# Windowed attention with 32 heads: one late copy of q's high parts, masks ahead of the rotation, and row maxima placed by small transfers

## The chip, the cores and the metric

The kernel runs on one core of a Trainium2 chip. Its engines are TensorE (PE, matmuls), VectorE (DVE), ScalarE (ACT), GpSimd (POOL) and SyncE (SP), which here only issues DMA transfers, each kind with an instruction queue of its own. The metric is the device time of one execution in microseconds. All intermediate data stay in SBUF, and TensorE writes to PSUM.

## The reference, cut to what matters

`x` is 8 x 512 x 256; 8 key/value heads serve 32 query heads of 64 columns, four query heads a group.

```python
xn = layernorm(x)
q = einsum('bqm,muh->bquh', xn, Wq) + bq;  k, v likewise with 8 heads
first  = even * cos - odd * sin            # interleaved rotation of q and k
second = odd * cos + even * sin
scores = einsum('bquh,bkuh->buqk', q * SCALE, k * SCALE)
scores = where(abs(pos_q - pos_k) <= 128, scores, -1e9)
probs  = softmax(concat([scores, sink]))[..., :-1]
s = einsum('buqk,bkuh->bquh', probs, v) @ Wo + bo
xq = (xn / scale).astype(float8_e4m3fn)    # scale from the largest |xn| of all
out = x + s * silu(xq @ weight.T + bias)
```

## The kernel before

**Steps and quarters.** The work is a software pipeline over 64 steps, one for each batch element and key/value group (`it = 8 * n + k`), with two filling steps ahead and one behind. Each step has four quarters `q`, one for each tile of 128 query positions. Within step `it`, TensorE projects the queries of step `it + 2` (quarter 0), forms the plain score rows of step `it + 1` (L1085, from which only each query's largest score is taken), forms the transposed scores of step `it` (L1108 and L1110, keys on the partitions), weighs the values with the exponentials (L1124), turns the head outputs (L1134) and projects them (L1147).

**Split numbers.** Scores are to have float32 accuracy, so each operand of the matmuls is split into a high part that the fast format holds exactly and a low remainder. `qT_full` holds, for 64 columns of q, the low parts on partitions 0 to 63 and the high parts on 64 to 127; against `kT_high`, which holds the keys' high parts twice, one matmul gives high x high and low x high (L1108). The third product needs q's high parts a second time, on partitions 0 to 63 of `qT_high`, against `kT_low` (L1110). Both q buffers have two halves, used by even and odd steps.

**The row maxima.** Before the exponential, each query's largest score is subtracted. VectorE finds it (L847), for two quarters (a pair) at a time, splits the negated maximum into two parts (`neg_parts`, 8 columns: two for each of four heads), TensorE turns these into 8 rows (L1067), and they are added by the same matmul L1110: `kT_low` has rows of ones on partitions 64 to 71, and `qT_high` has on partitions 64 to 71 the 8 rows. In a head's columns only its own two rows may be other than zero, so ScalarE copies the 8 rows four times, once for each head, each with a column of `own_rows` as scale that is one on the head's two rows and zero on the others (`max_rows`, L642 to L645). Pair 1 of step `it` is turned in quarter 0 of step `it`, pair 0 of step `it + 1` in quarter 2. The rows lie in PSUM bank `ring[2]`, which the turned head outputs need next: TensorE waits at L1209 and L1211 for ScalarE's copies.

**From projection to qT.** In a step, ScalarE takes the even and the odd columns out of PSUM (L616, L622), POOL rotates them (`turn_even` in quarter 0, `turn_odd` and `turn_rest` in quarter 1), ScalarE makes the high parts (`first_high` in quarter 1, `second_high` in quarter 2) and POOL the low ones (`first_low`, `second_low` in quarter 2). POOL also zeroes the corners of the exponentials that lie outside the window (`cut`, one or two blocks a quarter, L531), which the weighing of the next quarter needs. Within quarter 0, `turn_even` stands ahead of the mask, and waits until all six transfers of the step before have landed. Keys are made for four groups at once, twice in each batch element (k = 2 and 6): `keys_sum` in quarter 0 and `keys_low` in quarter 2 on POOL, `keys_high` in quarter 1 on ScalarE.

**SP's order.** SP executes its queue in order. In step `it` it sends the keys of step `t = it + 2` (six transfers of 64 KB, `keys_in`) and then the queries of step `a = it + 2` (`queries_in`): four transfers of 256 KB into `qT_full` (L376, L377) and two into `qT_high` (L381). `queries_in` first waits until the last score block of step `it` has been formed, since step `a` uses the same half. TensorE waits for the four and for the keys ahead of the first score row of the next step (L1074 to L1076). Where t is a multiple of four, the keys come from a freshly made group, and `keys_in` waits at L360 for POOL's `keys_low` of this same step. Results, and the loads of x, stand between at k = 0, 2 and 7.

```python
        sp.wait_ge(s_k_lo, 2 * quad + 2)               # L360, keys_in
        upto(sp, s_score_pe, NB * (a - 1))             # L372, queries_in; NB = 10 score blocks a step
        pool.wait_ge(s_even_done, a + 1)               # L468, turn_even
        upto(pool, s_qT_high_in, Q_IN * a)             # L471
```

## Time and profile before

| | |
|---|---|
| time, median of 3 runs | 2174.53 us (2162.39 to 2175.64) |
| profiled execution | 2158.91 us, its span 2157.2 us |
| granted TensorE clock, mean | 0.905 of full speed |
| busy: TensorE, VectorE, POOL, ScalarE | 85%, 59%, 47%, 41% of the span |
| DMA transfers of the kernel's queue | 44.6% of 16 engines' span |

The profile is one execution. Busy time of an engine is the time in its instructions; the rest it waits, for another engine's result or for a transfer. A timeline row gives the start, the duration, the engine, the line of the kernel, the operation with its output and inputs, and in brackets how long the engine had been idle before it and what ended that. "Issue" stands for an idle time whose end the profile ascribes to nothing. SPq is SP's issuing of transfers; the landing time of a transfer counts from its issue. A clock of 1.00 is 2.4 GHz, one of 0.50 is 1.2 GHz.

### The profile page before, as it was taken

Reading aid. Unit: us, or ns where it says so; the run is one execution under the profiler, and the core shown is the slowest. Engines: PE = TensorE matmul, PEld = TensorE weight load, DVE = VectorE, ACT = ScalarE, POOL = GpSimd, SP = SyncE. Lnnn points to the kernel's source line nnn. Section 1 sums busy time; section 2 is a strip of 40 time slices with the busy share of each in tenths; the row PEclk is TensorE's granted clock in tenths of the full one; section 3 lists DMA queues with packets and bytes.
Section 4 is the critical chain, followed back from the end, with each engine's and each line's share of the span. In section 5 each row is a group of like instructions: output and inputs, shape, how many; then the busy total and the mean of one; then the engine's idle time right before and its main releaser. Section 6 shows DMA issues by size and latency. Waiting matters only on the chain.

```text
span 2157.2 us, 33967 instructions
## 1 busy us (share of the span) xinstructions
PE 1823.1 (85%) x11139; PEld 1586.5 (74%) x11139; DVE 1272.2 (59%) x4156; ACT 886.5 (41%) x1893; POOL 1013.6 (47%) x1022
## 2 busy tenths in 40 slices
PE   2388888988989888988889888888898988898888
PEld 1177777777877777877777777777777777787777
DVE  8646556656656655655656655555665665565453
ACT  2134443444434444443444444343443444444343
POOL 4244444544635543553554554454463555355341
PEclk7579899999999988998999989898999998899899
DMA  4734443455255344445345344445425544534540
GB/s 151 129 47 59 62 67 59 79 84 70 40 85 77 64 65 68 68 61 91 52 60 94 57 64 67 63 76 84 65 43 87 77 66 63 74 56 58 91 64 13
DMA packets 92990, 150.89 MB, mean 70 GB/s; under 512 B 13712, under 2 KB 29840, under 8 KB 92816
## 3 DMA queue, kind: packets, MB, share of 16 engines
q1 hardware_dynamic: 92816, 148.72, 44.6%
q8 instruction: 91, 1.49, 0.3%
q14 instruction: 83, 0.68, 0.1%
HBM read 18.64 MB, written 4.19 MB: 11 GB/s over the span
## 4 chain that ended last, share of the span: by engine, by line
PE 48%; DMA 12%; issue 11%; POOL 9%; ACT 6%; SPq 5%; DVE 5%; POOLq 0%; DVEq 0%
PE pv_bank L1124 16%; DMA qT_high<-q_second_hi 7%; PE ring L1085 7%; PE acc L1147 6%; PE ring L1036 6%; PE score L1108 5%; PE score L1110 4%; DMA qT_full<-q_first_hi 4%; PE ring L1134 2%; POOL stage L531 2%; ACT qT_high L643 2%; ACT stage L610 2%; SPq L364 2%; SPq L376 1%; POOL q_second L473 1%
## 5 line engine op out<-in xcount | busy, mean ns | idle before, releaser
L847 DVE CUSTOM_DVE_ANT_0 junk<-ring,mask 128x384 bf16<-128x384 f32 (+1 forms) x1024 | 496.7, 488 | 696.5 <-PE ring L1085 687.7
L1124 PEld LDWEIGHTS pv_bank<-v,stage 128*128 128x128 f32 x5120 | 705.6, 206 | 30.2 <-issue 10.5
L1124 PE MATMUL pv_bank<-v,stage 128*128 128x65 f32 x5120 | 713.3, 282 | 10.8 <-ACT stage L610 3.8
L1085 PE MATMUL ring<-kT_high,qT_full 128*128 128x384 f32 (+1 forms) x1024 | 412.7, 404 | 219.6 <-issue 142.5
L610 ACT ACTIVATE stage<-score 128x512 f32<-128x512 f32 x640 | 356.8, 595 | 338.0 <-PE score L1110 337.3
L472 POOL TENSOR_TENSOR q_first<-q_even,cos 128x512 f32<-128x512 f32 x64 | 81.7, 1277 | 786.2 <-DMA qT_high<-q_second_hi 767.9
L1085 PEld LDWEIGHTS ring<-kT_high,qT_full 128*128 128x128 f32 x1024 | 213.7, 209 | 266.5 <-issue 178.7
L531 POOL TENSOR_SCALAR_AFFINE_SELECT stage<-stage 128x512 f32<-128x512 f32 x384 | 248.8, 663 | 232.5 <-ACT stage L610 231.5
L1108 PE MATMUL score<-qT_full,kT_high 128*128 128x512 f32 x640 | 279.6, 437 | 13.8 <-ACT stage L610 13.8
L643 ACT ACTIVATE qT_high<-ring,own_rows 8x256 fp32r<-8x256 f32 x512 | 196.3, 452 | 199.5 <-PE ring L1067 198.6
L1110 PE MATMUL score<-qT_high,kT_low 72*128 72x512 f32 x640 | 268.9, 420 | 0.0
L652 ACT ACTIVATE oT_hi<-ring 128x256 fp32r<-128x256 f32 x256 | 98.4, 384 | 391.1 <-PE ring L1134 391.1
L1108 PEld LDWEIGHTS score<-qT_full,kT_high 128*128 128x128 f32 x640 | 132.8, 207 | 66.4 <-ACT stage L610 49.0
L1036 PE MATMUL ring<-xT_hi,w_hi 128*128 128x512 f32 x320 | 142.8, 446 | 31.5 <-ACT q_even L616 22.6
L1147 PE MATMUL acc<-wo_hi,oT_hi 128*128 128x256 f32 x512 | 156.1, 305 | 0.5 <-DVE oT_lo L885 0.5
L1147 PE MATMUL acc<-wo_lo,oT_hi 128*128 128x256 f32 x512 | 155.7, 304 | 0.0
L1147 PE MATMUL acc<-wo_hi,oT_lo 128*128 128x256 f32 x512 | 155.1, 303 | 0.0
L1110 PEld LDWEIGHTS score<-qT_high,kT_low 72*128 72x128 f32 x640 | 132.3, 207 | 17.2
L885 DVE TENSOR_TENSOR oT_lo<-ring,oT_hi 128x256 fp32r<-128x256 f32 x256 | 108.7, 424 | 58.0 <-ACT oT_hi L652 53.8
L1036 PE MATMUL ring<-xT_hi,w_lo 128*128 128x512 f32 x320 | 127.8, 399 | 0.0
L1036 PE MATMUL ring<-xT_lo,w_hi 128*128 128x512 f32 x320 | 127.6, 399 | 0.0
L1134 PE MATMUL ring<-ident,o_norm 128*128 128x128 f32 x512 | 112.2, 304 | 18.0 <-ACT qT_high L643 17.3
(121 smaller groups left out, 2663.2 us busy)
## 6 DMA issues: line engine op xcount, KB each, us to landing
qT_full<-q_first SPq DMA_DIRECT2D x64, 256.0 KB, 4.2
qT_full<-q_first_hi SPq DMA_DIRECT2D x64, 256.0 KB, 5.6
qT_full<-q_second SPq DMA_DIRECT2D x64, 256.0 KB, 6.9
qT_full<-q_second_hi SPq DMA_DIRECT2D x64, 256.0 KB, 8.3
qT_high<-q_first_hi SPq DMA_DIRECT2D x64, 256.0 KB, 9.6
qT_high<-q_second_hi SPq DMA_DIRECT2D x64, 256.0 KB, 10.8
kT_high<-k_first_hi SPq DMA_DIRECT2D x128, 64.0 KB, 9.7
kT_high<-k_second_hi SPq DMA_DIRECT2D x128, 64.0 KB, 9.3
```

The lines of the kernel that those rows point to most:

```text
L531: nc.gpsimd.affine_select(out=pr, in_=pr, compare_op=ALU.is_ge, fill=0.0, base=0, pattern=[[0, GROUP], [sign, P]], channel_multiplier=-sign) \
L610: nc.scalar.activation(prob[:, q % 2 * 3 + n, :], score[(FIRST[q] + n) % 2][:, :], ACT.Exp) \
L643: last = nc.scalar.activation(qT_high[D:D + NR, s % 2, h, pair * 2 * P:(pair + 1) * 2 * P], ring[2][0:NR, 0:2 * P], ACT.Copy, scale=own_ro ...
L847: nc.vector.tensor_tensor_reduce(junk[:, h % 2, 0:cols], ring[h % 2][:, 0:cols], mask[:, m0:m0 + cols], 1.0, LOWEST, ALU.add, ALU.max, row ...
L885: nc.vector.tensor_tensor(oT_lo[:, q % 2, :], ring[2][:, 0:KT * P], oT_hi[:, q % 2, :].bitcast(F32), ALU.subtract).then_inc(s_oT_lo_done, 1)
L1036: last = nc.tensor.matmul(ring[1][:, :], w[:, k, col:col + P], xs[:, k, :], start=(n == 0), stop=(n == len(products) - 1))
L1085: nc.tensor.matmul(ring[h % 2][:, 0:cols], qT_full[:, b % 2, h, q * P:(q + 1) * P], kT_high[:, b % 3, k0 * P:k0 * P + cols], start=True, s ...
L1108: nc.tensor.matmul(score[blk % 2][:, :], kT_high[:, c % 3, k * P:(k + 1) * P], qT_full[:, c % 2, :, q * P:(q + 1) * P], start=True, stop=F ...
L1110: nc.tensor.matmul(score[blk % 2][:, :], kT_low[0:D + NR, c % 3, k * P:(k + 1) * P], qT_high[0:D + NR, c % 2, :, q * P:(q + 1) * P], start ...
L1124: last = nc.tensor.matmul(pv[:, h, :], prob[:, q % 2 * 3 + n, h * P:(h + 1) * P], v[:, slot, k, :], start=(n == 0), stop=(n == len(BLOCKS[ ...
L1134: last = nc.tensor.transpose(ring[2][:, k * P:(k + 1) * P], o_flat[:, k * P:(k + 1) * P], ident[:, :])
L1147: last = nc.tensor.matmul(acc[q // 2][:, (q % 2) * M:(q % 2 + 1) * M], left[:, q % 2, k * P:(k + 1) * P], right[:, col:col + M], start=fre ...
```

## The change

**The second copy of the high parts** is no longer two transfers from `q_first_hi` and `q_second_hi` behind the other four. SP copies partitions 64 to 127 of `qT_full` to 0 to 63 of `qT_high` in one transfer of 512 KB (`highs_in`), first thing in the next step, once the four have landed. `turn_even` no longer waits for the second copy, only for the four.

**The order on SP** becomes: high parts of step it + 1, keys (t not a multiple of four), small transfers for pair 1 of step it, result, small transfers for pair 0 of step it + 1, queries, keys (t a multiple of four), result.

**The row maxima.** ScalarE copies the 8 turned rows once, into `turned_rows`, when the small transfers of the pair before have landed. SP then sends each head's two rows (2 KB) to their place in `qT_high` (`rows_in`, four transfers). The other rows of `qT_high` on partitions 64 to 95 are zeroed once at the start by VectorE. TensorE's scores wait for the four transfers. `own_rows` and its two masks go.

**The order on POOL and ScalarE.** POOL masks quarter 0 ahead of `turn_even`; `first_low` and `second_low` follow `turn_rest` in quarter 1, `keys_sum` moves from quarter 0 to 2 and `keys_low` from 2 to 3. ScalarE's `second_high` moves from quarter 2 to 1 and `keys_high` from 1 to 3.

```diff
@@ SP
-                upto(sp, s_qT_high_in, Q_IN * a)
-                for row, _, high, _, _ in parts:
-                    sp.dma_start(qT_high[row:row + HALF, a % 2, :, :].bitcast(F32), high[:, :]) \
-                        .then_inc(s_qT_high_in, 16)
+            def highs_in(b):
+                sp.wait_ge(s_qT_first_in, Q_IN * (b + 1))
+                sp.wait_ge(s_qT_second_in, Q_IN * (b + 1))
+                upto(sp, s_qT_high_in, 16 * b)
+                sp.dma_start(qT_high[0:D, b % 2, :, :].bitcast(F32), qT_full[D:2 * D, b % 2, :, :].bitcast(F32)) \
+                    .then_inc(s_qT_high_in, 16)
+            def rows_in(s, pair):
+                sp.wait_ge(s_max_rows_done, 2 * s + pair + 1)
+                if s == 0 and pair == 0:
+                    sp.wait_ge(s_ones_ready, 3)
+                for h in range(GROUP):
+                    sp.dma_start(qT_high[D + 2 * h:D + 2 * h + 2, s % 2, h, pair * 2 * P:(pair + 1) * 2 * P]
+                                 .bitcast(F32), turned_rows[2 * h:2 * h + 2, :]).then_inc(s_rows_in, 16)
@@ SP, step
+                if real(b):
+                    highs_in(b)
                 if real(t) and t % QUAD:
                     keys_in(t)
+                if real(it):
+                    rows_in(it, 1)
                 if k == 0 and n >= 1:
                     result(n - 1, 0)
+                if real(it + 1):
+                    rows_in(it + 1, 0)
+                if real(a):
+                    queries_in(a)
                 if real(t) and t % QUAD == 0:
                     keys_in(t)
-                if real(a):
-                    queries_in(a)
@@ POOL
-                upto(pool, s_qT_high_in, Q_IN * a)
...
-                    if q == 0 and new_keys:
-                        keys_sum(quad)
-                    if q == 0 and real(a):
-                        turn_even(a)
-                    if q == 1 and real(a):
-                        turn_odd(a)
-                    if q == 2 and real(a):
-                        first_low(a)
-                    if real(it):
-                        cut(it, q)
-                    if q == 1 and real(a):
-                        turn_rest(a)
-                    if q == 2 and real(a):
-                        second_low(a)
-                    if q == 2 and new_keys:
-                        keys_low(quad)
+                    if q == 1 and real(a):
+                        turn_odd(a)
+                    if real(it):
+                        cut(it, q)
+                    if q == 0 and real(a):
+                        turn_even(a)
+                    if q == 1 and real(a):
+                        turn_rest(a)
+                        first_low(a)
+                        second_low(a)
+                    if q == 2 and new_keys:
+                        keys_sum(quad)
+                    if q == 3 and new_keys:
+                        keys_low(quad)
@@ ACT
-                for h in range(GROUP):
-                    last = nc.scalar.activation(qT_high[D:D + NR, s % 2, h, pair * 2 * P:(pair + 1) * 2 * P],
-                                                ring[2][0:NR, 0:2 * P], ACT.Copy, scale=own_rows[:, h:h + 1])
-                last.then_inc(s_max_rows_done, 1)
+                upto(act, s_rows_in, 16 * GROUP * (2 * s + pair))
+                nc.scalar.activation(turned_rows[:, :].bitcast(F32R), ring[2][0:NR, 0:2 * P], ACT.Copy) \
+                    .then_inc(s_max_rows_done, 1)
...
-                    if q == 2 and real(a):
-                        second_high(a)
...
                     if q == 1 and real(a):
                         first_high(a)
-                    if q == 1 and k in (2, 6) and quad < BATCH * QUADS:
+                        second_high(a)
+                    if q == 3 and k in (2, 6) and quad < BATCH * QUADS:
                         keys_high(quad)
@@ DVE, once
+            nc.vector.memset(qT_high[D:D + HALF, :, :, :].bitcast(F32), 0.0).then_inc(s_ones_ready, 1)
@@ PE, scores
-                    pe.wait_ge(s_qT_high_in, Q_IN * (c + 1))
+                    pe.wait_ge(s_qT_high_in, 16 * (c + 1))
-                    pe.wait_ge(s_max_rows_done, 2 * c + q // 2 + 1)
+                    pe.wait_ge(s_rows_in, 16 * GROUP * (2 * c + q // 2 + 1))
```

## Rows read from the trace of the kernel before

**Rows 1.** The page, part 1: engine, busy us, share of the span, instructions

```profile
PE 1823.1 (85%) x11139; PEld 1586.5 (74%) x11139; DVE 1272.2 (59%) x4156; ACT 886.5 (41%) x1893; POOL 1013.6 (47%) x1022
```

**Rows 2.** The waits: engine, line, what ended them, us in total, times, longest

```profile
POOL q_first L472 <- DMA qT_high<-q_second_hi: 767.9, 61, 17.5
PE ring L1085 <- issue: 142.5, 49, 7.1
PE ring L1134 <- ACT qT_high L643: 17.3, 47, 0.8
```

**Rows 3.** Timeline of an ordinary step: start, us, engine, line, operation, [idle before, releaser]

```profile
1008.71 0.40 PE L1110 MATMUL score<-qT_high,kT_low 72*128 72x512 f32 x1
...
1009.14 0.58 SPq L376 DMA_DIRECT2D qT_full<-q_first  x1
1011.06 0.61 SPq L377 DMA_DIRECT2D qT_full<-q_second_hi  x1
...
1019.38 0.36 PE L1085 MATMUL ring<-kT_high,qT_full 128*128 128x256 f32 x1 [1.98 <-issue]
```

**Rows 4.** Transfers of two steps, at 1102 and 1009: issuer, count, KB each, us to landing

```profile
qT_full<-q_second_hi SPq DMA_DIRECT2D x1, 256.0 KB, 8.3
kT_low<-k_second SPq DMA_DIRECT2D x1, 64.0 KB, 2.1
...
qT_high<-q_second_hi SPq DMA_DIRECT2D x1, 256.0 KB, 11.1
kT_low<-k_second SPq DMA_DIRECT2D x1, 64.0 KB, 8.6
```

**Rows 5.** Timeline of a fourth step, with the first and last of fifteen such waits

```profile
216.98 0.55 PE L1085 MATMUL ring<-kT_high,qT_full 128*128 128x256 f32 x1 [5.02 <-issue]
...
1101.26 1.28 POOL L511 TENSOR_TENSOR k_second<-k_second,k_second_hi 128x512 f32<-128x512 f32 x1
1101.61 0.40 PE L1110 MATMUL score<-qT_high,kT_low 72*128 72x512 f32 x1
1102.57 0.50 SPq L364 DMA_DIRECT2D kT_high<-k_first_hi  x1
1106.36 0.58 SPq L376 DMA_DIRECT2D qT_full<-q_first  x1
...
1116.64 0.55 PE L1085 MATMUL ring<-kT_high,qT_full 128*128 128x256 f32 x1 [5.94 <-issue]
...
2009.87 0.55 PE L1085 MATMUL ring<-kT_high,qT_full 128*128 128x256 f32 x1 [5.68 <-issue]
```

**Rows 6.** Timeline, ScalarE and the first score block of quarter 2

```profile
1000.14 0.63 ACT L627 ACTIVATE q_first_hi<-q_first 128x512 fp32r<-128x512 f32 x1
1004.60 1.53 ACT L643 ACTIVATE qT_high<-ring,own_rows 8x256 fp32r<-8x256 f32 x4 [0.85 <-PE ring L1067]
1011.86 0.38 ACT L652 ACTIVATE oT_hi<-ring 128x256 fp32r<-128x256 f32 x1 [2.09 <-PE ring L1134]
...
1030.26 0.39 PE L1108 MATMUL score<-qT_full,kT_high 128*128 128x512 f32 x1
```

**Rows 7.** Stretches with columns: busy us of each engine, granted clock, DMA share, GB/s

```profile
1019.10:1023.10 4.00, 3.27 (x24) 3.10 (x24) 1.37 (x7) 2.23 (x7) 0.00 (x0) 0.82 1.06 141
1114.00:1124.00 10.00, 7.36 (x33) 7.20 (x34) 3.58 (x13) 2.13 (x6) 3.45 (x4) 0.50 0.76 101
```

**Rows 8.** Timeline, POOL's first rotation of an ordinary step

```profile
1023.68 1.28 POOL L472 TENSOR_TENSOR q_first<-q_even,cos 128x512 f32<-128x512 f32 x1 [13.60 <-DMA qT_high<-q_second_hi]
```

**Rows 9.** Groups by line: matmuls of the weighing, busy us, mean ns, idle before by releaser

```profile
L1124 PE MATMUL pv_bank<-v,stage 128*128 128x65 f32 x5120 | 713.3, 282 | 10.8 <-ACT stage L610 3.8 <-DVE v L836 3.8 <-issue 1.8
```

**Rows 10.** Timeline of the start: DVE and SP

```profile
1.17 1.34 DVE L979 MEMSET kT_low<- 32x1536 f32 x1 [1.17 <-PEq L1301]
...
62.87 0.60 SPq L350 DMA_DIRECT2D x_res<-in_x  x1
...
74.73 1.41 DVE L711 BATCH_NORM_STATS2 stats<-x_res 128x6 f32<-128x256 f32 x4 [14.41 <-DMA x_res<-in_x]
```

20 lines of the change are left out of this document (7 added, 13 removed).

## The prediction

> **What bounds the kernel now.** I read the page's engine totals first, then the table of waits, then the timeline of a few steps, then the landing times of the transfers, and last the granted clock by windows. TensorE is busy for 85% of the span [rows 1]. No other engine is close, so a change is worth what it does to TensorE's own waits. POOL's wait of 768 us for the second q copy [rows 2] is the largest wait of all, and TensorE hardly feels it. Of TensorE's waits one stands out: 142.5 us in 49 waits ahead of the score rows L1085, released by nothing the profile names [rows 2]. The timeline names it. In an ordinary step the last score block starts at 1008.71 and takes 0.40, so it ends at 1009.11. SP issues the first q transfer 0.03 us later, because line 372 waits for exactly that block. The fourth is issued at 1011.06, and the rows start at 1019.38 after 1.98 us of idling [rows 3]. The fourth transfer lands 8.3 us after its issue [rows 4]: 1011.06 + 8.3 = 1019.36. So each step has a fixed distance of 10.3 us from the end of the last score block to the first row, of which TensorE's own work fills 8.3.
>
> Every fourth step the distance is longer. There SP must first send a group's keys: k_low ends at 1102.54, six key transfers go out from 1102.57, and the first q transfer leaves at 1106.36, 4.35 us after the last score block's end at 1102.01. The rows start at 1116.64, after a wait of 5.94 us. There are 15 such waits, the first 5.02 and the last 5.68 [rows 5], 83.8 us together. The other 34 make 58.7.
>
> **The change, part by part.**
>
> *Keys behind queries.* SP now sends q first and the fourth step's keys last, and the keys' conversion and low part move to quarter 3. q leaves at S + 0.03 (S is the end of the last score block) and has landed at S + 10.3. The keys: ScalarE reaches their conversion behind the head outputs of that quarter, which end 3.1 us after S in the ordinary step (1011.86 + 0.38), and two conversions of 0.63 take it to S + 4.4 [rows 6]. Two POOL subtractions of 1.28 [rows 5] take it to S + 6.95. Six issues at the spacing 0.64 put the last at about S + 10.15. On an empty queue a key transfer lands in 2.1 us, behind the q ones in 8.6 [rows 4]. The queue is empty of q by S + 10.3, so the last keys land at S + 12.2. Today's rows start at S + 14.6 here, and about 14.1 over the fifteen. Gain 1.9 x 15 = 28 us, taken as 27. Bounds: nothing, if something holds the keys 2 us longer; 83.8 - 15 x 2.0 = 54 us, if they come no later than q.
>
> *The clock.* After the wait of 5.9 us the granted clock is at its lower level, 1.2 GHz (0.50), for all of 1114 to 1124; around the 2 us wait it is 0.82 over four microseconds [rows 7]. A wait of 3.9 lies between. Most of those slow microseconds are no loss, since the rows there are paced by the maxima too. I take 0.3 us a time, 4 us; bounds 0 and 15 x 2.5 = 37 if a shorter wait keeps the full clock.
>
> *One ScalarE copy for four.* Four masked copies take 1.53 us together [rows 6], 0.38 each in the row; I allow 0.45 for a lone one. TensorE waits for them ahead of the head transposes 47 times, 17.3 us in all, never above 0.8 [rows 2]. 1.08 us less ends every one: 17 us. Bounds 15 and 18.
>
> *Four small transfers.* Each moves 2 KB. No row shows one; the issues shown take 0.50 to 0.61 us, whether of 64, 256 or 512 KB [rows 3, 5, 10], with 0.64 from one to the next, and a lone one of 64 KB lands in 2.1. For pair 0 the ScalarE copy starts at 1004.60 [rows 6], 4.5 us ahead of S. Copy 0.45 and four issues of 0.64 leave SP free for q 1.4 us before S. So nothing, hidden behind quarter 2's remaining matmuls; the cover is gone at 1.0 us an issue. For pair 1 the order on SP is: the q copy (issued when q has landed, S + 10.35), six keys in three steps of four (to S + 14.8), then the four (to S + 17.4), landing by about S + 19.5. TensorE wants them at 1030.26 [rows 6], which is S + 21.15. Cover about 1.7 us, so nothing again; in the fourth steps there are no keys in between and the cover is larger.
>
> *The second q copy, one transfer of 512 KB, a step later.* The sixth of today's q transfers is issued 1.3 us after the fourth and lands 11.1 us after its issue [rows 4], so the last two take 2.0 us each, 131 GB/s; at that rate it takes 4 us, S + 10.35 to about S + 16.5, while nothing else is wanted. Its reader is a step away. The Trainium skill, "SBUF — State Buffer", section on the DMA port swizzle, says partitions 0 to 31 and 32 to 63 share ports, so a transfer into 64 partitions has only half of them. By that rule the joined copy gains nothing in rate from its shape, and the sum stays as it is; whether it loses by reading only half the ports as well no run here shows. At half of today's rate it would end at S + 19 and push the four small transfers to about S + 21, just at the end of their cover, so the far bound is 0.5 us x 45 = 22 us.
>
> *Masking ahead of the rotation on POOL.* Today the rotation waits 13.60 us for the second copy and the quarter-0 mask stands behind it [rows 8]. TensorE's whole wait ahead of the weighing L1124 is 10.8 us, of which 3.8 is VectorE's values and 3.8 the exponentials [rows 9]. I take 3 us; bounds 0 and 7. The rotation starts 4 us sooner. What is late next is the second high part, now in quarter 1 on ScalarE: POOL delivers it at about S + 21.0, it ends at 21.65, and the next exponential is wanted at S + 22. Cost 0, bound 0.6 x 64 = 40 us if POOL is a microsecond slower. Where the low parts waited behind a mask they are now earlier; they were ready before S anyway.
>
> *Start and end.* The load of x that VectorE awaits for 14.41 us is issued at 62.87 behind six q transfers [rows 10]; two of those now come later: 2 x 2.0 = 4 us less. Behind the keys it may be issued 1 us later. The new memset is 4096 against 1536 columns at 1.34 us [rows 10], 3.5 us, of which 1 to 2 stand ahead of the first statistics. Net 3 us gained, bounds -3 and +6. The end is untouched.
>
> **Sum:** 27 + 4 + 17 + 3 + 3 = 54 us. The profiled execution took 2158.9 (span 2157.2), so it would become about 2105. The median of the runs is 2174.5, with 2162.4 the lowest; waits taken away subtract alike, so the median becomes **2120**.
>
> **The rivals.**
>
> *B, the keys only change places.* TensorE waits for keys as long as it waited for q behind keys. For it: the keys start 6.4 us later after S than today, and depend on ScalarE's last operation of the quarter. Against: the key transfers are short. Then 2174.5 - 23 = 2151. 15%.
>
> *C, slower: the small transfers hold SP.* The four for pair 0 stand directly ahead of q in SP's queue, in every step. If an issue of two rows takes 1.3 us and not 0.64, q leaves 4 x 1.3 + 0.45 - 4.5 = 1.2 us after S, and all of it reaches the 62 steps: 72 us, and pair 1 misses its cover as well, by about 1 us in 45 steps. It decides from 1.0 us an issue. 2120 + 72 = 2192, with the second part up to 2235. Against: every issue shown lies between 0.50 and 0.61 whatever its size [rows 3, 5, 10]. The Trainium skill, "DMA: Bandwidth & Descriptors", section on why a DMA increments its semaphore by 16, says that a transfer over two partitions runs on two engines and the issuing sequencer writes the other 14 increments itself. By that rule SP has extra work in each issue; no row here has such a transfer. 11%.
>
> *D, the gains don't add up.* VectorE's maxima and the clock take back what the copies give. For it: VectorE is busy for 59% of the span and sits in the loop of every row [rows 1]. About 2168, the gain under 1%. 12%.
>
> *E, q itself lands sooner.* If the two transfers now queued behind q slowed it, the 58.7 us of ordinary waits shrink too, and the clock stays up: 2120 - 50 = 2070. Against: two that follow take the same 2.0 us as those before them, in order. 10%.
>
> **How the numbers follow.** The forecast has 52%, the others as given. Range: the forecast's own is 2095 to 2145 (keys gain 0 to 54, ScalarE bound). To hold 8 in 10 it takes in B and most of D and a piece of E: 2078 to 2168. About 1% (22 us) is what a measurement of this kernel can tell. Faster by over 1%: forecast, E, and half of B, 0.70. Within: half of B, D, and a little of C, 0.20. Slower: 0.10.
>
> **What would show it.** After the change: POOL's wait at L472 down from 768 to under 600 and on a qT_full transfer; no TensorE wait for the max rows; first q transfer 0.03 us after S in all steps; waits ahead of L1085 of about 3.9 us in the fourth steps and an unchanged 2.0 elsewhere. Wrong would be: q issued later than S + 0.1 (C), fourth-step waits of 6 us (B), a new wait ahead of the first score block of quarter 2 (small transfers late), or ScalarE idling for q_second ahead of the exponentials.

## The result, and the profile after

| | before | after |
|---|---|---|
| time, median of 4 runs each | 2171.67 us (2162.39 to 2175.64) | 2068.95 us (2054.21 to 2074.46) |
| ratio | 1 | 0.9522, 95% interval 0.9463 to 0.9581 |
| profiled execution, span | 2158.91, 2157.2 us | 2074.46, 2072.7 us |
| granted TensorE clock, mean | 0.905 | 0.907 |

The kernel became 103 us faster. The forecast was 2120, its range 2078 to 2168, so the result lies below the range. A second run of the same kernel beside the first experiments gave 2078.24 us, ratio 0.9586 (0.9512 to 0.9661); it is named below where a comparison needs it. Ratios leave out two executions (one of the kernel before, one of a kernel below) that lay over 1.5% above the fastest of the same kernel.

I read the profile after in the order of the one before. First the engine totals, which answer to [rows 1]:

```profile
PE 1807.7 (87%) x11139; PEld 1592.2 (77%) x11139; DVE 1277.2 (62%) x4157; ACT 730.8 (35%) x1509; POOL 1011.2 (49%) x1019
```

ScalarE has lost 384 instructions and 156 us, the copies. POOL's busy time is the same. Then the waits, which answer to [rows 2] (line numbers are about 8 higher for TensorE, 11 for POOL):

```profile
POOL stage L542 <- ACT stage L619: 833.7, 193, 18.7
...
PE ring L1093 <- DMA kT_low<-k_second: 71.0, 16, 8.5
...
POOL q_first L483 <- DMA qT_full<-q_second_hi: 86.6, 45, 3.0
```

```profile
PE ring L1093 <- issue: 39.6, 31, 5.1
PE ring L1075 <- issue: 26.2, 39, 1.1
```

POOL's wait of 768 us ahead of the rotation has moved to the masks, which now stand ahead of it. TensorE's 142.5 us in 49 waits ahead of the score rows have become 71.0 + 39.6 = 110.6 in 47, and its waits for the ScalarE copy are gone. One line has grown: L1075, the turn of the row maxima, 18.7 to 26.2 us. I had not looked at it before.

The fourth step, timeline (start, us, engine, line, operation):

```profile
946.83 0.40 PE L1118 MATMUL score<-qT_high,kT_low 72*128 72x512 f32 x1
...
947.26 0.61 SPq L376 DMA_DIRECT2D qT_full<-q_first  x1
949.21 0.61 SPq L377 DMA_DIRECT2D qT_full<-q_second_hi  x1
...
952.73 1.29 POOL L522 TENSOR_TENSOR k_second<-k_second,k_second_hi 128x512 f32<-128x512 f32 x1
...
957.13 0.59 SPq L366 DMA_DIRECT2D kT_low<-k_second  x1
...
959.49 0.55 PE L1093 MATMUL ring<-kT_high,qT_full 128*128 128x256 f32 x1 [4.00 <-DMA kT_low<-k_second]
```

S, the end of the last score block, is 947.23. The first q transfer leaves at S + 0.03, the key subtraction ends at S + 6.8, the last key is issued at S + 9.9 and the row starts at S + 12.3, after a wait of 4.00 us. This is the forecast's course to within 0.3 us (3.9, S + 6.95, S + 10.15, S + 12.2). The landings (the page's part 6: issuer, count, KB each, us to landing):

```profile
qT_high<-qT_full SPq DMA_DIRECT2D x64, 512.0 KB, 4.5
qT_full<-q_first SPq DMA_DIRECT2D x64, 256.0 KB, 4.2
...
qT_full<-q_second_hi SPq DMA_DIRECT2D x64, 256.0 KB, 8.0
```

And the view that led to the cause which no part of the sum had, VectorE's groups by line. Before:

```profile
L862 DVE CAST neg_parts<-neg_max 128x8 fp32r<-128x8 f32 x128 | 48.1, 376 | 4.4
```

After:

```profile
L869 DVE CAST neg_parts<-neg_max 128x8 fp32r<-128x8 f32 x128 | 100.8, 787 | 4.4
```

The same copy of eight columns took 376 ns on average before and takes 787 now. It is one of four small VectorE operations (L865 to L872) between the last row maximum of a pair of quarters and TensorE's turn of the maxima; I call them the chain, and say that it is caught where one of them is held up by an operation of POOL. The first pair's chain follows quarter 1's rows, the second pair's follows quarter 3's. Timeline of a first-pair chain after, VectorE, then POOL:

```profile
1094.52 0.29 DVE L865 SCALAR_TENSOR_TENSOR neg_max<-row_max,neg_sink 128x8 f32<-128x8 f32 x1
1094.84 1.22 DVE L869 CAST neg_parts<-neg_max 128x8 fp32r<-128x8 f32 x1
1095.98 0.15 DVE L870 TENSOR_TENSOR sink_arg<-neg_max,neg_sink 128x8 f32<-128x8 f32 x1
1096.10 0.56 DVE L872 TENSOR_TENSOR neg_parts<-neg_max,neg_parts 128x8 fp32r<-128x8 f32 x1
1096.58 0.61 DVE L840 TENSOR_TENSOR v<-ring,v_bias 128x448 f32<-128x448 f32 x1
```

```profile
1094.75 1.28 POOL L507 TENSOR_TENSOR q_second<-q_second,q_second_hi 128x512 f32<-128x512 f32 x1
1095.99 1.23 POOL L542 TENSOR_SCALAR_AFFINE_SELECT stage<-stage 128x512 f32<-128x512 f32 x2
```

The CAST starts 0.09 us behind a POOL subtraction of two operands and ends with it (1096.06 and 1096.03). Sorted by what POOL does at its start, the 128 CASTs of the trace after take 0.17 us beside an idle POOL (51 of them), 0.37 beside a mask (2), and 1.22 beside a product or subtraction of 128x512 (75: the second low part L507 in 60 first-pair chains, the keys' low part L522 in 15 second-pair ones). Before, 69 had POOL idle, 13 a mask, 43 a 128x512 sum, product or difference at 0.7 on average (all in the first pair) and 3 a small operation.

The CAST alone understates what POOL did in the kernel before. In 21 of those 43 chains it had begun ahead of POOL's operation and was short, and the operation behind it was held up:

```profile
1093.93 0.75 DVE L858 SCALAR_TENSOR_TENSOR neg_max<-row_max,neg_sink 128x8 f32<-128x8 f32 x1
1094.71 0.17 DVE L862 CAST neg_parts<-neg_max 128x8 fp32r<-128x8 f32 x1
1094.79 1.25 DVE L863 TENSOR_TENSOR sink_arg<-neg_max,neg_sink 128x8 f32<-128x8 f32 x1
1095.96 0.15 DVE L865 TENSOR_TENSOR neg_parts<-neg_max,neg_parts 128x8 fp32r<-128x8 f32 x1
```

```profile
1093.38 1.27 POOL L485 TENSOR_TENSOR q_odd<-q_odd,cos 128x512 f32<-128x512 f32 x1
1094.73 1.28 POOL L487 TENSOR_TENSOR q_second<-q_second,q_odd 128x512 f32<-128x512 f32 x1
```

So the whole chain is the measure. From the start of its first operation to the end of its last, the first pair's takes 2.08 us on average before and 2.30 after, the second pair's 0.57 before and 0.96 after. The collision was there already; the change has not taken it away.

The Trainium skill, "SBUF — State Buffer", section "Who interferes with whom", states the rule: VectorE and GpSimd share a pair of SBUF ports, a VectorE instruction in a two-port mode or with two SBUF inputs takes it, and whoever comes second is blocked until the other's instruction is over. The trace agrees: the blocked CAST and the blocked difference end as POOL's operation does (the 1.25 us one at 1096.04, POOL's at 1096.01), not in proportion to their eight columns.

### The profile page after: what moved, and what is told of

Its sections match the earlier page's. It is cut to its first block, busy times and chain, and to the rows that moved or that the text cites. A ratio compares the mean times of both kernels' runs of the same rounds, so it can differ in the third digit from the quotient of the medians.

```text
span 2072.7 us, 34158 instructions
## 1 busy us (share of the span) xinstructions
PE 1807.7 (87%) x11139; PEld 1592.2 (77%) x11139; DVE 1277.2 (62%) x4157; ACT 730.8 (35%) x1509; POOL 1011.2 (49%) x1019
## 4 chain that ended last, share of the span: by engine, by line
PE 68%; issue 6%; DVE 6%; SPq 5%; ACT 4%; DMA 4%; POOL 3%; POOLq 0%; DVEq 0%
PE pv_bank L1132 23%; PE ring L1093 10%; PE acc L1155 8%; PE ring L1044 8%; PE score L1116 7%; PE score L1118 6%; PE ring L1142 3%; SPq L364 3%; ACT stage L619 2%; PE ring L1053 2%; DMA qT_full<-q_second_hi 2%; DMA kT_low<-k_second 2%; POOL k_first L520 1%; POOL k_second L522 1%; SPq L366 1%
## 5 line engine op out<-in xcount | busy, mean ns | idle before, releaser
L1044 PEld LDWEIGHTS ring<-xT_hi,w_hi 128*128 128x128 f32 x320 | 63.5, 199 | 71.7 <-ACT q_even L625 42.4
L886 DVE TENSOR_TENSOR o_norm<-pv_bank,rden 128x256 f32<-128x256 f32 x256 | 108.7, 425 | 9.3 <-DVE rden L883 0.5
```

Of the source, the lines that this page charges most:

```text
L886: nc.vector.tensor_tensor(o_norm[:, :, :], pv[:, :, 0:D], rden[:, :].rearrange("p (h a) -> p h a", a=1).broadcast_to([P, GROUP, D]), ALU.m ...
L1044: last = nc.tensor.matmul(ring[1][:, :], w[:, k, col:col + P], xs[:, k, :], start=(n == 0), stop=(n == len(products) - 1))
```

## The experiments

Each kernel ran in three rounds beside the kernel before on the same chip, so ratios to it are the measure. A difference between two kernels is given as the difference of their ratios times 2170 us; with intervals of 0.2 to 0.8% to either side it is good to some 10 to 20 us. The changed kernel stands at 0.9522 in the result and at 0.9586 in its repeat: against the repeat, every gain over after is 14 us larger and every loss 14 us smaller. In the sections on parts, "on after" means that one part of the change is undone, "on before" that one is made alone.

### What each part is worth

**The changed kernel again**, no edit: 0.9586, as told above.

> The changed kernel unaltered, timed on the same chip beside the kernel before and the three undoings. Expected by every theory: about 2069 us, 0.952 of before, with row waits of 3.95 to 4.8 us in the fourth steps and 1.75 us in the ordinary ones.

**Keys part undone, on after** (keys sent ahead of the queries, their sum in quarter 0, low part in 2, high in 1):

```
-                if real(a):
-                    queries_in(a)
                 if real(t) and t % QUAD == 0:
                     keys_in(t)
+                if real(a):
+                    queries_in(a)
```

> The changed kernel with the keys' part undone: in the fourth steps SP sends the keys ahead of the queries again, and keys_sum, keys_high and keys_low stand in quarters 0, 1 and 2. Theory T (each part is worth the TensorE wait that it takes away, plus a share of clock, and the parts add up): the fifteen fourth-step waits go back from 4.2 to about 5 to 6 us, so 15 to 27 us of waits and 5 us of clock, 2090 to 2100. Rival R (the surplus over my sum comes from coupling, POOL being early lets everything else run freely): POOL is now early anyway, so k_low is ready well before the last score block, q leaves on time or at most 1 us late, and the undoing costs under 8 us: below 2077.

Measured 2048.67 us (2032.36 to 2055.99), ratio 0.9441 (0.9364 to 0.9517): 18 us faster than after, 31 than its repeat on the same chip, each to some 20 us. The part that the forecast gave the largest term gains nothing in the changed kernel; by both comparisons it is rather a loss. With the new order of the queries' work the keys' low part ends 3.7 us ahead of S on average, q leaves between S + 0.03 and S + 2.7 (1.2 on average), and the fourth steps' wait is 3.04 us, less than the 4.2 of after. The keys' low part also leaves the second pair's chain, whose mean falls from 0.96 to 0.57 us.

**Four copies again, on after** (the one copy and the small transfers undone, the four masked copies back):

```
-                nc.scalar.activation(turned_rows[:, :].bitcast(F32R), ring[2][0:NR, 0:2 * P], ACT.Copy)
+                for h in range(GROUP):
+                    last = nc.scalar.activation(qT_high[D:D + NR, s % 2, h, pair * 2 * P:(pair + 1) * 2 * P],
+                                                ring[2][0:NR, 0:2 * P], ACT.Copy, scale=own_rows[:, h:h + 1])
```

> The changed kernel with the row maxima's part undone: ScalarE makes four masked copies again and there are no small transfers. Theory T: the 17 us of TensorE waits ahead of the head transposes come back, 2069 + 17 = 2086, with up to 5 us more of clock. Rival R (ScalarE's relief also shortened other waits, so that this part is worth 30 us or more): 2100 or more. Rival S (the small transfers hold SP and cost what the copies give): 2069 or less.

Measured 2120.25 us (2105.12 to 2127.94), ratio 0.9773 (0.9698 to 0.9847): 54 us slower than after, 41 slower than its repeat on the same chip. This is more than theory T's 2086; the time is rival R's.

**Second copy behind q again, on after**, as two transfers, with POOL's wait for them at the odd half's product:

```
+                if real(a):
+                    highs_in(a)
...
-                if real(b):
-                    highs_in(b)
```

> The changed kernel with the second copy of q's high parts as before: two transfers of 256 KB from q_first_hi and q_second_hi right behind the queries (in the fourth steps behind the keys); POOL waits for them ahead of turn_odd, not ahead of turn_even, and the mask stays ahead of the rotation. Theory T (q lands 0.25 us sooner and never a whole microsecond late, because nothing is queued behind it): ordinary row waits go back from 1.75 to 2.0 us with some of 3.0, the 34 waits from 39 to 59 us, 2069 + 20 = 2089. Rival R (the second copy mattered only through POOL's wait and the mask): row waits stay at 1.75 us, and the time at 2069 to 2075.

Measured 2127.94 us (2118.94 to 2138.27), ratio 0.9818 (0.9747 to 0.9889), 64 us slower than after, 50 slower than the repeat. In the two of every eight steps with the longest ordinary waits these went from 1.73 to 2.37 us on average, and the fourth q transfer lands 8.3 us after its issue, not 8.0: two transfers queued behind q do slow q. All ordinary waits went from 39.6 to 56.7 us, as theory T had them; its time of 2089 was 39 us too low. The time at the half clock is about 395 us here and about 320 in after (the measure is that of the section on waits below); why is not traced further.

**Keys part alone, on before:**

```
-                if real(t) and t % QUAD == 0:
-                    keys_in(t)
                 if real(a):
                     queries_in(a)
+                if real(t) and t % QUAD == 0:
+                    keys_in(t)
```

> The kernel before with the keys' part alone: in the fourth steps SP sends the queries first and the keys last, keys_sum, keys_high and keys_low stand in quarters 2, 3 and 3. Theory T2 (the keys' part is judged against POOL's lateness: it only pays where POOL is late, so the parts don't add up): fourth-step waits go from 5.6 to about 4 us, 15 x 1.6 = 24 us of waits and some clock, 2172 - 30 = 2142. Rival (the part costs 25 us whatever stands around it, as its undoing on the changed kernel suggests): 2172 to 2200.

Measured 2182.21 us (2175.01 to 2192.67), ratio 1.0085 (1.0054 to 1.0117), slower. TensorE's waits:

```profile
PE ring L1085 <- DMA kT_low<-k_second: 125.6, 16, 11.3
PE ring L1085 <- issue: 59.1, 34, 5.2
```

The keys now stand behind six q transfers and not four, and the fourth steps wait 7.6 us for them on average. This is rival B of the prediction, in a kernel without the late second copy, and the rival of this run.

**Queries' order on POOL and ScalarE undone, on after** (rotation ahead of the quarter-0 mask, low parts and the second high part in quarter 2):

```
+                    if q == 0 and real(a):
+                        turn_even(a)
                     if q == 1 and real(a):
                         turn_odd(a)
+                    if q == 2 and real(a):
+                        first_low(a)
                     if real(it):
                         cut(it, q)
-                    if q == 0 and real(a):
-                        turn_even(a)
                     if q == 1 and real(a):
                         turn_rest(a)
-                        first_low(a)
-                        second_low(a)
+                    if q == 2 and real(a):
+                        second_low(a)
```

> The changed kernel with the order on POOL and ScalarE of before for the queries: the rotation ahead of the quarter-0 mask, first_low and second_low around the quarter-2 mask, second_high in quarter 2. Keys and transfers as changed. Theory T2 (the mask's place is worth little, because the rotation now starts 4 us sooner by itself): no waits ahead of the weighing come back, 2075 to 2082. Rival (the order is where the surplus over my sum sits, through ScalarE's wait for the second high part ahead of the third exponentials): 2095 or more.

Measured 2015.5 us (2008.21 to 2027.13), ratio 0.9309 (0.9248 to 0.937): 46 us faster than after; neither theory nor rival had it. Of the first-pair CASTs 7 are now held up by a 128x512 difference and 18 stand beside a mask, where 60 were held up, and the chain's mean is 1.43 us, not 2.30. The second pair's 15 are caught as in after, at the keys' low part.

**The two transfer parts alone** (late second copy, one copy with small transfers):

> Keeps the joined late second copy and the one ScalarE copy with small transfers; the keys and the order of the queries' work on POOL and ScalarE stand as before the change. Theory (each of the two reorders costs by itself, keys about 27 us, queries' order about 57 us): 2072 - 27 - 57, about 1990 us, with the fourth steps' first q transfer at S + 1.2 and their row waits near 3.0 us, VectorE's negation chain back near 1.5 us. Rival (both reorders load the same POOL, so that undoing the second gives nothing more): 2010 to 2015 us, the time of the better of the two alone.

Measured 2037.38 us (2035.82 to 2038.39), ratio 0.9387 (0.9355 to 0.942). Neither theory had it. Set beside the runs above it shows that the parts don't add: on these two the keys part gives 17 us (0.9387 to 0.9309), beside the new order it costs 18 (0.9441 to 0.9522); the new order costs 12 without it (0.9387 to 0.9441) and 46 with it. The gap of 34 us between these is good to some 26; the 17, 18 and 12 by themselves are hardly more than the intervals leave open.

**The late second copy alone, on before:**

> The kernel before with the late, joined second copy alone. Theory (the late second copy frees POOL's turn of the queries, so the fourth steps' keys are ready before S, and the queue behind q is shorter): fourth-step waits from 5.6 us to about 3, 15 x 2.6 = 39 us and the clock with them, so 2170 - 50 = 2120 or less. Rival (the gain of the late copy exists only beside the new order on POOL): within 15 us of the time before, 2155 to 2175, with the keys' low part still ending after S + 0.4.

Measured 2054.77 us (2044.99 to 2068.34), ratio 0.948 (0.9418 to 0.9542), 113 us faster than before by itself. The way that the theory gave is wrong: the keys are no earlier (low part at S - 0.8, q at S + 3.2 on average; before, S - 0.6 and S + 3.4) and the fourth steps still wait 5.0 us. POOL's rotation starts at S + 10.1 in ordinary steps and not at S + 14.2, and the first pair's chain takes 1.18 us on average and not 2.08.

**One copy and small transfers alone, on before:**

> The kernel before with one ScalarE copy and small transfers alone; the two second copies stay behind the queries and POOL waits for them as before. Theory (TensorE's wait for the maxima's rows goes, 17.3 us, and the clock and the rows behind it give about as much again): 2170 - 35 to 45, about 2130. Rival one (the copies are worth only their 17 us as in the forecast): 2153. Rival two (the small transfers stand ahead of q in SP's queue and cost what the copies give): 2170 or above.

Measured 2157.1 us (2152.12 to 2157.83), ratio 0.9929 (0.9908 to 0.9951): 15 us. Rival one, the forecast's 17, is the nearest.

So, in the order in which the parts were stacked: late second copy -113, one copy and small transfers -20, keys -17, new order on POOL and ScalarE +46; together -104 us.

### POOL beside VectorE's chain

**POOL's second low part behind the chain, on after.** One wait more, nothing moved:

```
                 pool.wait_ge(s_second_hi, a + 1)
+                upto(pool, s_neg_done, 2 * (a - 1) + 1)
                 nc.gpsimd.tensor_tensor(q_second[:, :], q_second[:, :], q_second_hi[:, :], ALU.subtract)
```

> The changed kernel with one wait added: POOL's subtraction for the second low part waits until VectorE's four small operations on the negated maxima of pair 0 are done. The order on every engine stays. Theory (POOL's 128x512 subtraction and VectorE's small operations with two operands in SBUF exclude each other; 60 of 64 of the chains of pair 0 are caught, 1.05 us each, and TensorE and its clock pay more than once over): CAST mean from 0.79 to about 0.3 us, time 2069 - 50, about 2015 to 2025. Rival (the order of mask and rotation costs by making the mask or the exponentials late, and the stretched operations are a mere sign): 2060 to 2075, with the CAST short all the same.

Measured 1986.72 us (1973.52 to 1992.05), ratio 0.9151 (0.9101 to 0.9201): 80 us faster than after, from a wait, and 30 below the theory, which had counted the CAST alone. The same place in the step, VectorE, then POOL:

```profile
1036.24 0.29 DVE L866 SCALAR_TENSOR_TENSOR neg_max<-row_max,neg_sink 128x8 f32<-128x8 f32 x1
1036.56 0.17 DVE L870 CAST neg_parts<-neg_max 128x8 fp32r<-128x8 f32 x1
1036.64 0.16 DVE L871 TENSOR_TENSOR sink_arg<-neg_max,neg_sink 128x8 f32<-128x8 f32 x1
1036.77 0.17 DVE L873 TENSOR_TENSOR neg_parts<-neg_max,neg_parts 128x8 fp32r<-128x8 f32 x1
```

```profile
1037.09 1.29 POOL L508 TENSOR_TENSOR q_second<-q_second,q_second_hi 128x512 f32<-128x512 f32 x1 [0.58 <-DVE neg_parts L873]
```

From the start of the first operation to the end of the last the chain takes 0.70 us here and 2.14 in the timeline of after; over all first pairs 0.76 and 2.30. POOL idles 0.58 us for it, and its result is wanted only at S. TensorE's wait at the turn of the maxima, 26.2 us in after, is gone but for 1.9 us at one place.

**A useless POOL product beside the chain, and the same behind it**, on the kernel with the queries' order undone:

```
+                    if q == 1 and real(it + 1):
+                        beside_chain(it + 1)
...
+                pool.wait_ge(s_max_done, TILES * GROUP * b + 2 * GROUP)
+                nc.gpsimd.tensor_tensor(pool_junk[:, :], cos[:, :], sin[:, :], ALU.mult)
```

The second kernel waits for `s_neg_done, 2 * b + 1` instead.

> The kernel with the order of mask, rotation and low parts as before the change (2015.5 us) and one useless POOL product of 128x512 a step, which starts when the last maximum of pair 0 is there, beside VectorE's small operations. Theory: the chain is caught in about 63 steps, CAST mean near 0.7 us, time 2015 + 40 to 55, about 2060. Rival (small operations' length is off the path): 2015 to 2022.

> As the run with the useless product beside the chain, but the product waits until the chain is done. Same work on POOL, some tenths of a us later. Theory: the chain is free, 2015 to 2025 us. Rival (POOL's extra 1.3 us a step costs by itself): the same as with the product beside the chain.

Measured 2121.28 us (2118.32 to 2133.28), ratio 0.9791 (0.9743 to 0.9839), beside the chain; 1994.25 us (1989.73 to 2000.66), ratio 0.9196 (0.9147 to 0.9245), behind it. The work is the same, the place differs by a microsecond, and 129 us lie between. The CAST's group, first beside, then behind:

```profile
L880 DVE CAST neg_parts<-neg_max 128x8 fp32r<-128x8 f32 x128 | 95.6, 747 | 4.4
```

```profile
L880 DVE CAST neg_parts<-neg_max 128x8 fp32r<-128x8 f32 x128 | 37.8, 296 | 4.4
```

Beside it TensorE waits at the turn of the maxima:

```profile
PE ring L1086 <- issue: 43.4, 45, 1.7
```

Behind it the kernel is even 25 us faster than without the useless product (0.9196 against 0.9309): waiting for the chain also takes the real differences out of its way, none of the 64 first-pair chains is caught. 129 us is more than the theory's 55; over 64 chains it is 2.0 us each. In the trace beside the chain each chain meets not only the useless product but also the first low part behind it, which holds the CAST in 48 of them, and the whole chain takes 2.65 us on average against 0.57 behind it, 2.08 us more. TensorE's waits of the 43.4 us line are gone behind the chain but for 0.9 us, and the time at the half clock is about 400 us beside it and about 220 behind it; half of that difference is 90 us. So the cost is in part TensorE's wait and in larger part the slow matmuls behind it.

The first pair's chain from its first start to its last end, and how many of the 64 take over 1 us:

| kernel | mean, us | over 1 us | ratio |
|---|---|---|---|
| before | 2.08 | 56 | 1 |
| before, only POOL's wait moved (below) | 1.28 | 32 | 0.9688 |
| before, late second copy | 1.18 | 25 | 0.948 |
| two transfer parts | 1.32 | 31 | 0.9387 |
| after without the queries' order | 1.43 | 37 | 0.9309 |
| after | 2.30 | 61 | 0.9522 |
| after, low part behind the chain | 0.76 | 7 | 0.9151 |
| useless product beside the chain | 2.65 | 63 | 0.9791 |
| useless product behind it | 0.57 | 0 | 0.9196 |

Between kernels that differ only in where POOL's work meets the chain (the last four rows, pairwise) time and chain move together; across kernels with other transfers the chain is one term among several.

**Only POOL's wait moved, on before** (all transfers stay):

```
 def turn_even(a):
-                upto(pool, s_qT_high_in, Q_IN * a)
...
 def turn_odd(a):
                 pool.wait_ge(s_odd_done, a + 1)
+                upto(pool, s_qT_high_in, Q_IN * a)
```

> The kernel before with a single edit: POOL's wait for the second q copy stands ahead of the odd half's product in quarter 1, where its buffer is first written, and no longer ahead of the even half's in quarter 0. All transfers stay as before. Theory (the late second copy was worth 115 us by itself because POOL's rotation and the quarter-0 mask came 4 us earlier, out of the way of VectorE's chain): most of it, 2060 to 2090 us. Rival (it was worth that because two transfers less stand behind q in SP's queue): within 20 us of before, 2150 to 2175.

Measured 2101.88 us (2093.23 to 2107.69), ratio 0.9688 (0.9642 to 0.9733): between theory and rival, nearer to the theory. 68 us of the late copy's 113 come from POOL's work being 4 us earlier. The first-pair chains that take over 1 us fall from 56 to 32, and their mean by 0.80 us, 51 us over 64 steps; TensorE's waits ahead of the rows fall by 9 us and those ahead of the weighing from 10.8 to 0.4. The other 45 us (good to some 17) come with the two transfers off q's queue: TensorE's waits ahead of the rows are 133.7 us here and 116.0 with the late copy, and in the ordinary steps with the longest waits (two of every eight) they fall from 2.4 to 1.76.

**The guard put into the kernel before:**

```
+                upto(pool, s_neg_done, 2 * (a - 1) + 1)
                 nc.gpsimd.tensor_tensor(q_odd[:, :], q_odd[:, :], cos[:, :], ALU.mult)
```

> The kernel before with one wait added and nothing moved: POOL's last two operations of the rotation (and so the first low part behind them) wait until VectorE's small operations on the maxima of pair 0 are done. POOL still waits for the second q copy in quarter 0. Theory (the overlap is the cost): 2170 - 60 to 90, about 2095, below what the earlier wait for the second copy gave. Rival (the late rotation makes the high and low parts and with them q's transfers late): 2150 or above, with the first q transfer no longer 0.03 us behind the last score block.

Measured 2278.88 us (2270.05 to 2284.41), ratio 1.0525 (1.0484 to 1.0567), 114 us slower, although no first-pair chain is caught. The time lies where the rival had it, "2150 or above", but not by its mechanism: q still leaves at S + 0.03 in the ordinary steps. Both missed the queue behind the product. The waits of this kernel:

```profile
PE ring L1135 <- ACT qT_high L644: 125.3, 103, 2.3
```

```profile
ACT q_second_hi L632 <- POOL q_second L488: 156.7, 63, 4.8
```

```profile
POOL q_odd L486 <- DVE neg_parts L866: 156.1, 63, 7.2
```

POOL's rotation is delayed behind the chain; ScalarE's second high part waits for it, and in ScalarE's order the copies of the row maxima stand behind that. TensorE waits for them 125.3 us, where it was 17.3 [rows 2]. A wait is free only where its product has slack. On after the product was the second low part, wanted two quarters later; here it was one that ScalarE was about to ask for.

### What a wait of TensorE costs beyond its length

**Useless matmuls in the row waits, on after.** They compute nothing and begin when the wait does: 17 of 512 columns in the fourth steps, 6 in two of the other four of every eight.

```
+                    if q == 0 and real(b) and b % 8 in (0, 4, 5, 6) and b > 1:
+                        idle_filled(b, 17 if b % 4 == 0 else 6)
                     row(0)
```

> The changed kernel with useless matmuls in TensorE's idle time ahead of the first score row: 17 of 512 columns (3.7 us) in the fourth steps, 6 (1.3 us) in the two classes of steps with a 1.75 us wait. They write a bank that the score row overwrites; nothing else is changed and no work is saved. Theory C (the granted clock multiplies each wait: 169 of the 321 slow microseconds follow these waits and cost 0.3 to 0.65 us each): the clock stays at 2.4 GHz through these quarters, slow time falls by 130 us or more, and the time by 40 to 80 us, to 2000 to 2035. Rival D (the slow microseconds lie beside VectorE's maxima and cost nothing, the surplus is elsewhere): 2070 to 2080, or above if the matmuls overrun.

Measured 2021.19 us (2017.29 to 2030.38), ratio 0.9335 (0.9269 to 0.9402): 41 us less than after, with no transfer earlier: theory C's range. The mean granted clock rose from 0.907 to 0.946. Summed over windows of one microsecond from 115 us on, the time at the half clock fell from about 320 to about 150 us; half of the difference, 85 us, is what that stretch of matmuls takes less, and part of it lies beside other waits.

**Real work put there instead** (the output product and the first weighing ahead of row 0 of quarter 0):

> The changed kernel with useful work moved into the same idle time: in quarter 0 the output projection (6 matmuls, 1.4 us) and the first head's weighing go ahead of the first score row. Theory C: the ordinary waits of 1.75 us vanish, the fourth-step waits fall from 4.1 to 2.3, 34 + 27 = about 60 us of idle, and half as much again by the clock: 2075 - 90 = 1985. Rival D (idle time only): 2075 - 60 = 2015. Rival F (VectorE's maxima start no sooner and become the bound): 2060.

Measured 2064.76 us (2050.13 to 2066.93, and 2084.84 in the execution left out), ratio 0.9513 (0.944 to 0.9586), no change. The waits ahead of row 0 (from step 1 on) fall from 102.0 to 61.1 us, but the first score block of quarter 2 now waits for the small transfers of the row maxima, where after had 1.8 us in 4 waits:

```profile
PE score L1116 <- DMA qT_high<-turned_rows: 24.4, 24, 2.2
```

The rows start later behind the work put ahead of them, and with them the maxima. That this is what makes the small transfers late is argued, not tested. Rival F's 2060 is the nearest.

**The filler on the two transfer parts, and on the guarded kernel** (11 and 6 matmuls, 17 and 6):

> The kernel with the transfers only, and useless matmuls of 512 columns in TensorE's row waits: 11 in the fourth steps and 6 in two of the other four of every eight, each begun only when the wait begins; they compute nothing. Theory (a wait costs its length and then a stretch at the half clock): less slow clock, about 30 to 45 us below the same kernel without them, so 1945 to 1960. Rival (the clock falls for another reason than these waits, and the matmuls delay the rows): the same time or 10 us more.

> The best one so far (POOL's second low part behind VectorE's small operations, 1986.7 us) with useless matmuls of 512 columns in TensorE's row waits: 17 in the fourth steps, 6 in two of the other four of every eight, begun only when the wait begins; they compute nothing. Theory (each wait costs its length and then slow clock): 48 us less as in the two pairs run before this, 1935 to 1950. Rival (with the chain free there is little slow clock left to win): 1970 to 1987.

Measured 1989.08 us (1983.18 to 1992.48), ratio 0.9162 (0.9126 to 0.9198), and 1936.14 us (1934.42 to 1937.83), ratio 0.8935 (0.8909 to 0.8962). The filler gives 41, 49 and 47 us on three kernels, the last as the theory had it. The last one beats both kernels of the case, by 231 and 127 us. Span and clock of the guarded kernel without and with it:

```profile
core 0: 1987.5 us, clock 0.929
```

```profile
core 0: 1936.1 us, clock 0.964
```

## Why the prediction was wrong, point by point

**The step that failed first** is the part on the second q copy: a step later, "while nothing else is wanted", it was counted only for its own transfer time, and POOL's wait of 768 us for it was put down as one that "TensorE hardly feels". Leaving q's queue was worth 113 us by itself and stood in the sum with 0. TensorE does not feel the wait. It feels where POOL's work lands after it. POOL's rotation, masks and low parts fill about 14 us a step, and the wait pushed the rotation's end to where VectorE prepares the maxima. The trace of before showed it, in the CAST's mean of 376 ns for eight columns against 178 for a reciprocal of four, and more plainly in the first pair's chain of 2.08 us beside the second pair's of 0.57. I costed only queues and results, not what two engines do to each other while both have work. 68 us of the 113 come with POOL's earlier work, by the run that moved the wait alone; the shorter chains (51 us) and fewer waits ahead of rows and weighing make them up.

**What that leaves of the sum.** In the changed kernel the collision is back: its first-pair chain takes 2.30 us, so what the late copy took out of the chain the new order put in again, and the two don't show in the total. In the profiled executions the gain is 84 us, where the sum had 54. TensorE's waits account for most of it: 21 in the fourth steps, 19 in the ordinary ones, 17 for the copies, 10 ahead of the weighing, 5 at the start, less 7 at the turn of the maxima. The ordinary waits are the term that stood at nothing. Some 19 us are not traced.

**Rival E was real.** The other 45 us came with the two transfers gone from behind q; 18 of them are waits ahead of the rows. I gave it 10% on the ground that transfers go in order. Those that follow do slow the earlier ones: the fourth q transfer lands 8.0 us after its issue, not 8.3, and the ordinary waits went from 58.7 us in 34 to 39.6 in 31.

**Masking ahead of the rotation, +3:** wrong in sign. The weighing's wait did go, from 10.8 us [rows 9] to 0.6, but it is 0.6 too with the mask behind the rotation in the changed kernel, and 0.4 with the late copy alone: POOL's earlier start ended it, and the mask's place gave nothing. And the low parts, which the text called "now earlier; they were ready before S anyway", landed on the chain's CAST in 60 of 64 steps, and the group cost 46 us. With one wait more the same order is at 0.9151, against 0.9309 with the old one without the wait; but the old order whose chain is free, useless product and all, is at 0.9196, so that the new order itself gains is not shown.

**The keys, 27 us:** the course was right to 0.3 us, and the fourth steps' waits fell from 83.9 to 62.5 us. With the earlier POOL and the old order the measured gain is 17. In the changed kernel as it is the part came out as a loss of 18 us, near the edge of the intervals; what it was priced against, the fourth steps' low part ending on average only 0.6 us ahead of S, is no longer true there: without the part it ends at S - 3.7 and the fourth steps wait 3.04 us, not 4.2. I priced against the old timing a part that stands beside another part which changes it.

**One copy for four, 17 us:** measured 15 alone, 20 on the late copy, 41 to 54 in the changed kernel. TensorE's wait for it is gone, as forecast. Why undoing it costs so much more there is not settled; the time at the half clock goes from about 320 to about 375 us with it, and half of the difference, 27 us, is a part.

**The small transfers, 0, and rival C:** the cover held. An issue takes 0.58 us on average (0.61 for a q transfer), q leaves at S + 0.03 in all steps, and TensorE waits 1.8 us for them, in 4 waits. The cover is thin, as reckoned: with other work ahead of the rows the waits for them were 24.4 us. The Trainium skill, "DMA: Bandwidth & Descriptors", in the section on why a DMA increments its semaphore by 16, had the issuing sequencer write increments itself; in the issues' length this does not show.

**The clock, 4 us:** the mean clock did not move (0.905 to 0.907), so the term was about right in the sum and by chance. Its price was not: I took a wait to cost little beyond its length, and filling waits with matmuls gave 41 us for waits that did not become shorter.

**Rate of the joined copy:** 512 KB between two ranges of 64 partitions land in 4.5 us where 256 KB of a q transfer need 4.2, so it loses nothing, and the bound of 22 us fell away. The start gained 5.3 us (first row of step 1 at 109.0, before 114.3), 3 forecast; with the keys part undone it is at 113.6, with the late copy alone at 111.0, so the parts don't add here either.

**The range** was 90 us wide and all its cases took after's gains as a sum over queues. None had POOL and VectorE excluding each other, and that moved the time by up to 129 us in the runs above, more than the whole forecast of 54.

## What to carry to other kernels

Look for an instruction whose mean duration is too long for its shape: if a small VectorE operation in a chain that TensorE waits for is longer than its like, lay POOL's timeline beside it, time the whole chain and not one of its operations, and hold POOL's two-operand work back until the chain is done, but only work whose result has slack and has no engine's queue behind it. Price each part of a change against the timeline that the other parts leave, not the old one. An engine's wait that nobody feels can still decide where its work lands.

## What the runs showed of the hardware

- An eight-column VectorE CAST takes 0.17 us beside an idle POOL, 0.37 to 0.56 on average beside a mask of 128x512 (which reads one operand), and 1.22 when it begins behind a product or difference of 128x512. A small VectorE operation of two operands is held up alike (0.15 to 0.16 us alone, 1.25 in the lines above); one that begins first is not. VectorE operations with one operand in PSUM, as the 128x256 low part of the head outputs, take 0.42 us in either case.
- The collisions with 64 chains cost 80 us on the changed kernel, where they made the chain 1.54 us longer, and 129 us where two POOL operations in a row made it 2.08 us longer: 1.3 and 2.0 us a step.
- The fourth of four transfers of 256 KB lands 8.0 us after its issue when nothing is queued behind it, and 8.3 with two more behind.
- A transfer of 512 KB from 64 partitions to 64 others lands in 4.5 us, one of 256 KB from 128 partitions to 32 in 4.2.
- Matmuls that compute nothing, put into TensorE's waits, made three kernels faster by 41, 49 and 47 us.
